# A fused decoder layer in fp32: a pair's products in the order keys, values, queries, and the query features after the sums

## The chip, the cores and the metric

The kernel runs on one core of a Trainium2 chip. The metric is the device time of one execution, in microseconds (us). The core has five engines that run side by side and meet only at semaphores: TensorE (PE, matrix products into PSUM banks), VectorE (DVE), ScalarE (ACT), GpSimd (POOL) and SyncE (SP, which issues the DMAs). Each engine runs its own instructions strictly in the order of the program; an instruction that waits holds everything behind it on its engine.

## What is computed

A decoder layer on x of shape (16, 128, 256): a stack of 8 attention and feed-forward layers, then a cross attention with a context, then a mixture of 8 experts. The change is in the stack alone. For each of the 8 layers:

```python
Q  = elu(x @ Wq + bq) + 1;  Kf = elu(x @ Wk + bk) + 1;  V = x @ Wv + bv   # 16 heads of 64
KV = sum(Kf * V, over the sequence);  sumK = sum(Kf, over the sequence)
att = Q * KV / (Q * sumK + 1e-6)                 # elementwise: one number per channel
x = layernorm(gelu(att @ Wo + bo) + x)
h = gelu(gelu(x @ W1 + b1) @ W2 + b2)            # 256 -> 1024 -> 256
x = layernorm(h + x)
```

The feature elu(u)+1 equals max(u + 1, exp(min(u, 0))), which is how the kernel makes it.

## The kernel before

**Tiles and stages.** The 16 sequences are cut into 4 tiles of 4 sequences (512 tokens); 8 layers times 4 tiles are 32 tiles, numbered g = 0 to 31 in the order in which they run. The 1024 channels of the heads are 8 chunks of 128, handled as 4 pairs p = 0 to 3. Inputs and weights are split into a high and a low part (XTHI and XTLO, WHI and WLO, X1HI and X1LO, W1HI and W1LO), so that one product of a chunk is 6 matmuls of 512 columns, and the product of one kind (keys, values or queries) of a pair is 12.

**A slot.** The function slot exists once for each engine, and slot(l, t) is one step of a software pipeline over three tiles: the projections, features and sums of tile g+1; the output product (Wo), the first layer norm and the hidden layer of tile g; the down product (W2S) and second layer norm of tile g-1. On PE (L819 to L882) a slot runs: pair 0; half of the Wo product (8 chunks for blocks 0 and 2, the last two chunks after a wait for the weighted attention `att` of pair 3); pair 1; the other half of Wo, which completes Y and signals y_mm; pair 2; half of W2S; pair 3; three quarters of the other half of W2S, the transposes of R (the input of the hidden layer), the last quarter; hidden_start (the 8 matmuls of hidden chunks 0 and 1 with X1HI), hidden_rest for these two (4 matmuls with X1LO), the transposes of the input of tile g+2, and hidden chunks 2 to 7.

**Banks.** PS has six PSUM banks: keys in KB = 0 and 1, queries in QB = 2 and 3, values in VB = 4 and 5. A product of the next pair may overwrite its bank only when DVE has used it: keys wait for kf, queries for wq, values for kv_mul. Pairs are called with pair(p, 0, 2, 1): keys, queries, values. The hidden chunks use QB + m % 4: chunks 0 and 1 the two query banks (hidden_start waits for wq of pair 3), 2 and 3 the two value banks (they wait for kv_mul of pair 3), 4 to 7 the same four again behind ACT's gelus.

**ACT, a pair.** clip_keys (two relus of 512 elements from PSUM, L942), clip_queries (two more, L950, then one exponential over keys and queries together, 2048 elements, L954). invert takes the logarithm and the exponential of the denominators (L962, L964), weigh makes att in 8 small instructions (L977). In a slot the order is: invert(3) and weigh(3) of tile g around pair 0; clip_keys(1), invert(0), clip_queries(1), weigh(0); the gelu of Y; pair 2; invert(1); pair 3; weigh(1); invert(2); the copy X1HI (L1054); XTHI (L987); the gelus of the hidden layer with weigh(2) between them. The ACT engine also copies next layer's weights to WHI (high_parts, L923), in one slot of every four two of these just ahead of X1HI.

**DVE, a pair.** features: subtract 1 and add 1 again on the exponentials of the keys (called snap, L1096, from SBUF to SBUF), key features kf (two, L1102), the same for the queries (L1104, and L1108 gives wq, two). sums_of: key features times values, kv_mul (two, L1118), and one reduction over 2048 elements (L1125). denominators: three small instructions, the addition of ES to the query features (L1138), two small ones. newton: two instructions on the inverse (L1150, L1154). The order in a slot, which is written out by hand at L1214 to L1260:

```python
features(nl, nt, 2)
newton(nl, nt, 1)
sums_of(nl, nt, 2, normed1=norm1)        # kv_mul, layer norm of R, then the reduction
denominators(nl, nt, 2)
features(nl, nt, 3)
newton(nl, nt, 2, between=g if tile else None)   # X1LO between its two instructions
sums_of(nl, nt, 3, biased2=...)          # kv_mul, T<-Y,B, then the reduction
denominators(nl, nt, 3)
```

Ahead of it stand pair 0, features of pair 1, T<-Y,BO (called biased, L1174, which waits for y_mm), sums_of and denominators of pair 1, and the residual and the statistics of the first layer norm (L1179 to L1189).

**POOL** does the scale and the shift of both layer norms on 128 x 1024 elements (L663, L665, L700, L702) as soon as DVE has normed, and the low parts of next layer's weights (L626, L638). SP loads weights; none of its work changes.

Of the kernel before, what the change touches and what calls it, by code (L numbers as in the profile page):

```python
# [18 lines left out]
ACT = mybir.ActivationFunctionType  # L19
# [9 lines left out]
TILES = SEQS // TS  # L29
# [417 lines left out]
def attention_stack(nc, X, ident, cross, ffn, a, cross_loads, x, Wkvq, bkvq, Wo, bo, s1, c1, W1, b1, W2, b2, s2, c2):  # L447

    with ExitStack() as ctx:
# [3 lines left out]
        def sem(name):  # L453
            return ctx.enter_context(nc.semaphore(name))
# [42 lines left out]
        KB, QB, VB = 0, 2, 4  # L497
# [11 lines left out]
            sem(n) for n in ("w_hi", "b_neg", "clipped", "ex", "log", "inv", "y_act", "x1_hi", "h_act", "z_act", "xt_hi"))  # L509

# [231 lines left out]
        def _(pe):  # L742
# [49 lines left out]
            def hidden_start(l, t, g):  # L792

                if t == 0:
                    pe.wait_ge(w_lo, (l + 1) * PIECES)
                chunks = (g + 2) * HC if exists(l, t + 1) else LAST * HC
                for m in range(2):
                    pe.wait_ge(wq, chunks - 1 + m)
                    for kc in range(KD):
                        nc.tensor.matmul(PS[:, QB + m, :], W1HI[:, m, kc, :], X1HI[:, kc, :], start=(kc == 0), stop=False)  # L800
                        nc.tensor.matmul(PS[:, QB + m, :], W1LO[:, m, kc, :], X1HI[:, kc, :], start=False, stop=False)

            def hidden_rest(l, t, g, chunks):

                last = (g + 2) * HC if exists(l, t + 1) else LAST * HC
                for m in chunks:
                    if m < 2:
                        for kc in range(KD):
                            ins = nc.tensor.matmul(PS[:, QB + m, :], W1HI[:, m, kc, :], X1LO[:, kc, :], start=False,
                                                   stop=(kc == KD - 1))  # L810
                        ins.then_inc(h_mm, 1)
                        continue
                    if m < 4:
                        pe.wait_ge(kv_mul, last - 3 + m)
                    else:
                        pe.wait_ge(h_act, g * HC + (m - 3))
                    split_product(PS[:, QB + m % 4, :], W1HI[:, m], W1LO[:, m], X1HI, X1LO).then_inc(h_mm, 1)

            def slot(l, t):  # L819
# [13 lines left out]
                pair(0, 0, 2, 1)  # L833
# [9 lines left out]
                pair(1, 0, 2, 1)  # L843
                if tile:
                    down(WO, ATT, (1, 3)).then_inc(y_mm, 1)
                pair(2, 0, 2, 1)
# [9 lines left out]
                pair(3, 0, 2, 1)  # L856
# [59 lines left out]
        def _(act):  # L916
# [9 lines left out]
            def clip_keys(l, t, p):  # L926
# [13 lines left out]
                for i in range(2):  # L940
                    act.wait_ge(k_mm, 2 * n + i + 1)
                    nc.scalar.activation(EX[:, b, 2 + i, :], PS[:, KB + i, :], ACT.Relu, scale=-1.0,  # L942
                                         bias=BNEG[:, 0, 2 * p + i:2 * p + i + 1])

            def clip_queries(l, t, p):
# [8 lines left out]
                nc.scalar.activation(EX[:, b, 2:6, :], EX[:, b, 2:6, :], ACT.Exp, scale=-1.0).then_inc(ex, 1)  # L954
# [39 lines left out]
            def hidden(l, t, g, between, before):  # L994
                if t == 0:
                    act.wait_ge(b1_in, (l + 1) * 16)
                for m in range(HC):
                    act.wait_ge(h_mm, g * HC + (m + 1))
                    nc.scalar.activation(H[:, m, :], PS[:, QB + m % 4, :], ACT.Gelu_apprx_tanh,  # L999
# [88 lines left out]
        def _(dve):  # L1088
# [3 lines left out]
            def features(l, t, p):  # L1092

                n, b = (l * TILES + t) * PAIRS + p, p % 2
                dve.wait_ge(ex, n + 1)
# [4 lines left out]
                for i in range(2):  # L1100
                    c = 2 * p + i
                    nc.vector.scalar_tensor_tensor(EX[:, b, 2 + i, :], PS[:, KB + i, :], BUP[:, 0, c:c + 1],  # L1102
                                                   EX[:, b, 2 + i, :], ALU.add, ALU.max).then_inc(kf, 1)
                nc.vector.tensor_scalar(EX[:, b, 4:6, :], EX[:, b, 4:6, :], -1.0, 1.0, ALU.add, ALU.add).then_inc(snap, 1)  # L1104
# [22 lines left out]
            def denominators(l, t, p):  # L1127
# [6 lines left out]
                nc.vector.reciprocal(ES[:, b, :], sumk).then_inc(stat, 1)  # L1134
                dve.wait_ge(wq, 2 * n + 2)
# [824 lines left out]
```

## Time and profile before

| what | value |
|---|---|
| median of 3 runs | 2939.05 us (2930.69 to 2939.1) |
| the profiled execution's own time | 2939.07 us |
| its span (first to last instruction) | 2937.3 us |
| PE busy | 2820.4 us, 96% |
| DVE busy | 2388.0 us, 81% |
| ACT busy | 1919.4 us, 65% |
| POOL busy | 778.5 us, 27% |
| mean granted clock of TensorE | 0.979 |

The stack takes the span from its start to about 2450 us; cross attention and experts follow. The profile says of each engine how long it worked, but the matmuls are pipelined and their ends are modelled: whether PE waits is read from the distance between the starts of successive matmuls. In the table of the timeline the first number is the start, the second the duration. The chain that ended last is no help here, since it lies in the experts.

### The profile page before, as it was taken

To read this page: it belongs to the slowest core of one execution; us is meant where nothing else is said; L and a number is where in the kernel's file an instruction comes from. 1 tells how busy PE (TensorE), PEld (TensorE's weight loads), DVE (VectorE), ACT (ScalarE), POOL (GpSimd) and SP (SyncE) were. 2 spreads that over 40 slices of the span, in tenths; PEclk is the share of its full clock that TensorE was granted. 3 is DMA by queue.
4 is the path that set the end of the run, shared out by engine and by line. 5 is a ranking of instruction groups with operands and counts; after the bars stand their busy time and mean duration, and the time that the engine had idled before them with its cause. 6 is when DMAs were issued, how large, how long until landed. Compare 5 with 4: busy or idle time off the path is not lost. (4 is left out here: it accounts for less than half of the span.)

```text
span 2937.3 us, 35493 instructions
## 1 busy us (share of the span) xinstructions
PE 2820.4 (96%) x13018; PEld 2331.9 (79%) x13018; DVE 2388.0 (81%) x3583; ACT 1919.4 (65%) x2835; POOL 778.5 (27%) x512
## 2 busy tenths in 40 slices
PE   5799999999999999999999999999999999997989
PEld 4688888888888888888888888888888877775877
DVE  7878898889888988898888888888888875654366
ACT  4667777776777777777777777767767763443255
POOL 4002231223122312321233123312331124432313
PEclk9899999999999999999999999999999999997999
DMA  4000001000100010101010100110010010102322
GB/s 142 1 1 23 24 17 37 22 22 19 36 21 24 19 36 11 33 19 36 12 33 19 37 7 24 32 37 6 22 35 20 1 58 15 50 1 101 122 43 36
DMA packets 62093, 92.00 MB, mean 31 GB/s; under 512 B 16480, under 2 KB 42336, under 8 KB 59744
## 3 DMA queue, kind: packets, MB, share of 16 engines
q1 hardware_dynamic: 57840, 85.46, 9.2%
q0 software_dynamic: 4080, 4.27, 0.9%
q8 instruction: 104, 1.70, 0.2%
q14 instruction: 69, 0.57, 0.1%
HBM read 80.24 MB, written 10.38 MB: 31 GB/s over the span
## 5 line engine op out<-in xcount | busy, mean ns | idle before, releaser
L746 PE MATMUL PS<-XTHI,WHI 128*128 128x512 f32 x1536 | 625.8, 407 | 24.5 <-DVE EX L1102 18.9
L748 PE MATMUL PS<-XTHI,WLO 128*128 128x512 f32 x1536 | 608.1, 396 | 0.0
L747 PE MATMUL PS<-XTLO,WHI 128*128 128x512 f32 x1536 | 603.6, 393 | 0.0
L977 ACT ACTIVATE ATT<-INV,CC,CE 128x128 f32<-128x128 f32 x1024 | 432.4, 484 | 122.7 <-PE Y L788 116.5
L788 PE MATMUL Y<-WO,ATT 128*128 128x256 f32 x2048 | 454.6, 380 | 6.6 <-ACT ATT L977 6.6
L788 PE MATMUL Y<-W2S,H 128*128 128x256 f32 x2048 | 458.0, 379 | 2.0 <-DVE T L1174 1.4
L788 PEld LDWEIGHTS Y<-WO,ATT 128*128 128x128 f32 x2048 | 389.7, 190 | 63.2 <-ACT ATT L977 6.2
L788 PEld LDWEIGHTS Y<-W2S,H 128*128 128x128 f32 x2048 | 386.2, 190 | 56.3 <-DVE T L1174 1.8
L643 POOL TENSOR_TENSOR RSTD<-MV,EPS 128x4 f32<-128x4 f32 x68 | 16.3, 239 | 1346.8 <-DVE MV L1189 1337.5
L746 PEld LDWEIGHTS PS<-XTHI,WHI 128*128 128x128 f32 x1536 | 291.8, 190 | 89.7 <-issue 21.6
L942 ACT ACTIVATE EX<-PS,BNEG 128x512 f32<-128x512 f32 x256 | 165.7, 685 | 299.2 <-DVE INV L1154 156.4
L747 PEld LDWEIGHTS PS<-XTLO,WHI 128*128 128x128 f32 x1536 | 291.7, 190 | 64.7
L748 PEld LDWEIGHTS PS<-XTHI,WLO 128*128 128x128 f32 x1536 | 291.3, 190 | 65.0
L1150 DVE TENSOR_TENSOR EX<-EX,INV 128x1024 f32<-128x1024 f32 x128 | 161.8, 1264 | 164.3 <-ACT INV L964 164.3
L1125 DVE TENSOR_REDUCE SUMS<-EX 128x16 f32<-128x2048 f32 x128 | 292.1, 2282 | 2.3
L954 ACT ACTIVATE EX<-EX 128x2048 f32<-128x2048 f32 x128 | 245.0, 1914 | 4.1
L1138 DVE TENSOR_TENSOR EX<-EX,ES 128x1024 f32<-128x1024 f32 x128 | 223.3, 1744 | 13.7 <-DVE ES L1134 0.5
L962 ACT ACTIVATE INV<-EX 128x1024 f32<-128x1024 f32 x128 | 135.0, 1055 | 109.1 <-DVE EX L1138 108.7
L1096 DVE TENSOR_SCALAR EX<-EX 128x1024 f32<-128x1024 f32 x128 | 138.6, 1083 | 76.3 <-ACT EX L954 76.3
L1102 DVE SCALAR_TENSOR_TENSOR EX<-PS,BUP,EX 128x512 f32<-128x512 f32 x256 | 180.4, 746 | 5.7
L1108 DVE SCALAR_TENSOR_TENSOR EX<-PS,BUP,EX 128x512 f32<-128x512 f32 x256 | 180.5, 747 | 4.6
L999 ACT ACTIVATE H<-PS,B 128x512 f32<-128x512 f32 x256 | 177.5, 694 | 9.4 <-PE PS L748 5.0
(200 smaller groups left out, 4839.1 us busy)
## 6 DMA issues: line engine op xcount, KB each, us to landing
STAGE<-L_attn_Wkvq SPq DMA_DIRECT2D x64, 384.0 KB, 3.2
WO<-L_attn_Wo SPq DMA_DIRECT2D x8, 1024.0 KB, 4.8
W2S<-L_attn_W SPq DMA_DIRECT2D x8, 1024.0 KB, 4.7
STAGE<-L_attn_W SPq DMA_DIRECT2D x32, 256.0 KB, 5.5
WGU<-L_ffn_r_gate SPq DMA_DIRECT2D x8, 512.0 KB, 9.6
WGU<-L_ffn_r_up SPq DMA_DIRECT2D x8, 512.0 KB, 9.7
WD<-L_ffn_r_down SPq DMA_DIRECT2D x8, 512.0 KB, 9.6
rows_in<-R SPq DMA_DIRECT2D x1, 3036.0 KB, 14.0
```

The source lines that it names most:

```text
L746: nc.tensor.matmul(out, whi[:, kc, :], xhi[:, kc, :], start=(kc == 0), stop=False)
L747: nc.tensor.matmul(out, whi[:, kc, :], xlo[:, kc, :], start=False, stop=False)
L748: ins = nc.tensor.matmul(out, wlo[:, kc, :], xhi[:, kc, :], start=False, stop=(kc == KD - 1))
L788: ins = nc.tensor.matmul(Ytm[:, b, :], src[:, c, b * P:(b + 1) * P], w[:, c, :], start=(c == 0), stop=(c == HC - 1))
L942: nc.scalar.activation(EX[:, b, 2 + i, :], PS[:, KB + i, :], ACT.Relu, scale=-1.0, bias=BNEG[:, 0, 2 * p + i:2 * p + i + 1])
L954: nc.scalar.activation(EX[:, b, 2:6, :], EX[:, b, 2:6, :], ACT.Exp, scale=-1.0).then_inc(ex, 1)
L977: ins = nc.scalar.activation(ATT[:, 2 * p + i, ss], INV[:, b, i, ss], ACT.Identity, scale=CE[:, b, k:k + 1], bias=CC[:, b, k:k + 1])
L999: nc.scalar.activation(H[:, m, :], PS[:, QB + m % 4, :], ACT.Gelu_apprx_tanh, bias=B1[:, m:m + 1]).then_inc(h_act, 1)
L1102: nc.vector.scalar_tensor_tensor(EX[:, b, 2 + i, :], PS[:, KB + i, :], BUP[:, 0, c:c + 1], EX[:, b, 2 + i, :], ALU.add, ALU.max).then_inc( ...
L1108: nc.vector.scalar_tensor_tensor(EX[:, b, 4 + i, :], PS[:, QB + i, :], BUP[:, 2, c:c + 1], EX[:, b, 4 + i, :], ALU.add, ALU.max).then_inc( ...
L1125: nc.vector.tensor_reduce(SUMS[:, b, :], by_seq(EX[:, b, 0:4, :]), AX.X, ALU.add).then_inc(sums, 1)
L1138: nc.vector.tensor_tensor(q, q, spread(ES[:, b, :], SEQ), ALU.add).then_inc(denom, 1)
```

## The change

In the stack, and nowhere else:

- PE runs a pair as keys, values, queries (pair(p, 0, 1, 2)). The value banks become 2 and 3, the query banks 4 and 5. The hidden layer's chunks keep banks 2 to 5, so chunks 0 and 1 now lie in the value banks and wait for kv_mul, chunks 2 and 3 lie in the query banks and wait for wq.
- ACT makes the exponential of the keys by itself after the relus of the keys, and that of the queries after the relus of the queries; there are two new semaphores, clipped_k and ex_k.
- On DVE the query half of features becomes query_features and is called from denominators, after the reduction and the reciprocal, ahead of the addition of ES. The order of the calls in the slot stays.

```diff
-        KB, QB, VB = 0, 2, 4
+        KB, VB, QB = 0, 2, 4
+        clipped_k, ex_k = sem("clipped_k"), sem("ex_k")
...
                 for m in range(2):
-                    pe.wait_ge(wq, chunks - 1 + m)
+                    pe.wait_ge(kv_mul, chunks - 1 + m)
...
-                        nc.tensor.matmul(PS[:, QB + m, :], W1HI[:, m, kc, :], X1HI[:, kc, :], start=(kc == 0), stop=False)
-                        nc.tensor.matmul(PS[:, QB + m, :], W1LO[:, m, kc, :], X1HI[:, kc, :], start=False, stop=False)
+                        nc.tensor.matmul(PS[:, VB + m, :], W1HI[:, m, kc, :], X1HI[:, kc, :], start=(kc == 0), stop=False)
+                        nc.tensor.matmul(PS[:, VB + m, :], W1LO[:, m, kc, :], X1HI[:, kc, :], start=False, stop=False)
...
                     if m < 4:
-                        pe.wait_ge(kv_mul, last - 3 + m)
+                        pe.wait_ge(wq, last - 3 + m)
...
-                    split_product(PS[:, QB + m % 4, :], W1HI[:, m], W1LO[:, m], X1HI, X1LO).then_inc(h_mm, 1)
+                    split_product(PS[:, VB + m % 4, :], W1HI[:, m], W1LO[:, m], X1HI, X1LO).then_inc(h_mm, 1)
...
-                pair(0, 0, 2, 1)
+                pair(0, 0, 1, 2)
...
-                    nc.scalar.activation(EX[:, b, 2 + i, :], PS[:, KB + i, :], ACT.Relu, scale=-1.0,
-                                         bias=BNEG[:, 0, 2 * p + i:2 * p + i + 1])
+                    ins = nc.scalar.activation(EX[:, b, 2 + i, :], PS[:, KB + i, :], ACT.Relu, scale=-1.0,
+                                               bias=BNEG[:, 0, 2 * p + i:2 * p + i + 1])
+                ins.then_inc(clipped_k, 1)
+                act.wait_ge(clipped_k, n + 1)
+                nc.scalar.activation(EX[:, b, 2:4, :], EX[:, b, 2:4, :], ACT.Exp, scale=-1.0).then_inc(ex_k, 1)
...
-                nc.scalar.activation(EX[:, b, 2:6, :], EX[:, b, 2:6, :], ACT.Exp, scale=-1.0).then_inc(ex, 1)
+                nc.scalar.activation(EX[:, b, 4:6, :], EX[:, b, 4:6, :], ACT.Exp, scale=-1.0).then_inc(ex, 1)
...
-                dve.wait_ge(ex, n + 1)
+                dve.wait_ge(ex_k, n + 1)
...
+            def query_features(l, t, p):
+
+                n, b = (l * TILES + t) * PAIRS + p, p % 2
+                dve.wait_ge(ex, n + 1)
                 nc.vector.tensor_scalar(EX[:, b, 4:6, :], EX[:, b, 4:6, :], -1.0, 1.0, ALU.add, ALU.add).then_inc(snap, 1)
                 dve.wait_ge(snap, 2 * n + 2)
...
                 nc.vector.reciprocal(ES[:, b, :], sumk).then_inc(stat, 1)
+                query_features(l, t, p)
                 dve.wait_ge(wq, 2 * n + 2)
                 dve.wait_ge(stat, n * 4 + 2)
```

The gelu of the hidden layer (L999) reads its bank as VB + m % 4 instead of QB + m % 4.

## Rows read from the trace of the kernel before

**Rows 1.** Page, busy time of the engines: us, share of the span, instructions
```profile
PE 2820.4 (96%) x13018; PEld 2331.9 (79%) x13018; DVE 2388.0 (81%) x3583; ACT 1919.4 (65%) x2835; POOL 778.5 (27%) x512
```
**Rows 2.** Busy by stretch, one slot: stretch, length, busy by engine, clock, DMA share, GB/s
```profile
1054.88:1128.81 73.93, 73.84 (x338) 61.85 (x336) 65.04 (x97) 52.15 (x77) 12.69 (x8) 1.00 0.06 20
```
**Rows 3.** Timeline of PE, that slot: start us, duration us, engine, line, operation
```profile
1085.00 0.58 PE L746 MATMUL PS<-XTHI,WHI 128*128 128x512 f32 x1
...
1090.69 0.39 PE L746 MATMUL PS<-XTHI,WHI 128*128 128x512 f32 x1
...
1105.85 0.39 PE L746 MATMUL PS<-XTHI,WHI 128*128 128x512 f32 x1
...
1116.38 0.58 PE L800 MATMUL PS<-X1HI,W1HI 128*128 128x512 f32 x1
...
1120.47 0.48 PE L746 MATMUL PS<-X1HI,W1HI 128*128 128x512 f32 x1
...
1128.81 0.39 PE L746 MATMUL PS<-XTHI,WHI 128*128 128x512 f32 x1
```
**Rows 4.** Page, costliest groups, two of ACT: busy us, mean ns of one
```profile
L954 ACT ACTIVATE EX<-EX 128x2048 f32<-128x2048 f32 x128 | 245.0, 1914 | 4.1
...
L962 ACT ACTIVATE INV<-EX 128x1024 f32<-128x1024 f32 x128 | 135.0, 1055 | 109.1 <-DVE EX L1138 108.7
```
**Rows 5.** Timeline of ACT, the same slot and one with weight copies
```profile
1085.47 3.20 ACT L977 ACTIVATE ATT<-INV,CC,CE 128x128 f32<-128x128 f32 x8 [3.82 <-PE Y L788]
...
1106.05 0.69 ACT L950 ACTIVATE EX<-PS,BNEG 128x512 f32<-128x512 f32 x1 [0.68 <-PE PS L748]
...
1108.60 3.17 ACT L977 ACTIVATE ATT<-INV,CC,CE 128x128 f32<-128x128 f32 x8
...
1115.03 1.01 ACT L1054 CAST X1HI<-PS 128x1024 fp32r<-128x1024 f32 x1 [0.89 <-PE PS L866]
...
1189.89 1.55 ACT L923 CAST WHI<-STAGE 128x768 fp32r<-128x768 f32 x2
```
**Rows 6.** Timeline of DVE, the same slot, pairs 1 to 3
```profile
1085.79 1.22 DVE L1174 TENSOR_TENSOR T<-Y,BO 128x1024 f32<-128x1024 f32 x1
...
1088.35 2.29 DVE L1125 TENSOR_REDUCE SUMS<-EX 128x16 f32<-128x2048 f32 x1
...
1090.88 0.20 DVE L1134 RECIPROCAL ES<-SUMS 128x8 f32<-128x8 f32 x1
...
1092.61 1.22 DVE L1179 TENSOR_TENSOR R<-T,X 128x1024 f32<-128x1024 f32 x1
...
1095.40 0.28 DVE L1189 BATCH_NORM_AGGREGATE MV<-ST 128x2 f32<-128x6 f32 x3
...
1098.81 0.68 DVE L1104 TENSOR_SCALAR EX<-EX 128x1024 f32<-128x1024 f32 x1
...
1100.85 1.22 DVE L1150 TENSOR_TENSOR EX<-EX,INV 128x1024 f32<-128x1024 f32 x1
...
1105.85 2.28 DVE L1125 TENSOR_REDUCE SUMS<-EX 128x16 f32<-128x2048 f32 x1
...
1108.82 3.15 DVE L1138 TENSOR_TENSOR EX<-EX,ES 128x1024 f32<-128x1024 f32 x1
...
1117.38 1.22 DVE L1164 TENSOR_TENSOR X1LO<-PS,X1HI 128x1024 fp32r<-128x1024 f32 x1
...
1119.65 1.41 DVE L1118 SCALAR_TENSOR_TENSOR EX<-PS,BA,EX 128x512 f32<-128x512 f32 x2
```
**Rows 7.** Timeline of POOL, the shift of the first layer norm in that slot
```profile
1108.52 2.36 POOL L702 TENSOR_TENSOR R<-R,LN1P 128x1024 f32<-128x1024 f32 x1
```
**Rows 8.** Waits of the whole span: engine, line, waited for, us in total, times, longest
```profile
PE PS L746 <- DVE EX L1102: 18.9, 4, 6.7
```
**Rows 9.** Timeline of PE near the stack's end, a long wait
```profile
2409.59 3.62 PE L788 MATMUL Y<-WO,ATT 128*128 128x256 f32 x10 [3.69 <-ACT ATT L977]
```
**Rows 10.** Busy by stretch just behind that wait: the last but two is the clock
```profile
2410.70:2414.10 3.40, 3.40 (x10) 2.69 (x9) 0.00 (x0) 0.14 (x1) 1.75 (x1) 0.50 1.12 374
```

More of the change, by code:

```diff
@@ L808, in hidden_rest @@
                         for kc in range(KD):
-                            ins = nc.tensor.matmul(PS[:, QB + m, :], W1HI[:, m, kc, :], X1LO[:, kc, :], start=False,
+                            ins = nc.tensor.matmul(PS[:, VB + m, :], W1HI[:, m, kc, :], X1LO[:, kc, :], start=False,
                                                    stop=(kc == KD - 1))
@@ L842, in slot @@
                     down(WO, ATT, (0, 2), range(HC - 2, HC))
-                pair(1, 0, 2, 1)
+                pair(1, 0, 1, 2)
                 if tile:
                     down(WO, ATT, (1, 3)).then_inc(y_mm, 1)
-                pair(2, 0, 2, 1)
+                pair(2, 0, 1, 2)
                 if before:
@@ L855, in slot @@
                     down(W2S, H, (0, 1))
-                pair(3, 0, 2, 1)
+                pair(3, 0, 1, 2)
                 if before:
@@ L998, in hidden @@
                     act.wait_ge(h_mm, g * HC + (m + 1))
-                    nc.scalar.activation(H[:, m, :], PS[:, QB + m % 4, :], ACT.Gelu_apprx_tanh,
+                    nc.scalar.activation(H[:, m, :], PS[:, VB + m % 4, :], ACT.Gelu_apprx_tanh,
                                          bias=B1[:, m:m + 1]).then_inc(h_act, 1)
```

## The prediction, made before the changed kernel ran

> **What bounds the kernel now.** I read the busy times first: PE is busy 96% of the span, DVE 81%, ACT 65% [rows 1]. Busy matmuls say little by themselves, so I took one slot of the stack by stretch and by timeline. It lasts 73.93 us, of which PE is busy 73.84, DVE 65.04 and ACT 52.15 [rows 2]. In it the products follow each other without a hole: from the first start of pair 3's third product to hidden_start 10.53 us, to hidden chunk 2 14.62, to the next slot's first product 22.96 [rows 3]. So in the stack PE sets the pace and nothing else does; whatever the change takes off another engine's path is worth nothing there, and every wait that it puts in front of PE is paid in full, in each of the 31 slots that also project a next tile (g = 0 to 30). What may be gained is the start of the stack, where PE waits for key features, 18.9 us in four waits [rows 8]. DVE has 8.9 us to spare a slot, ACT 21.8 [rows 2]: DVE's order matters nearly as much as PE's.
>
> **The change, part by part.** *The exponential.* One of 1.914 us becomes two of 1.055 [rows 4]: ACT gains 0.2 us of work a pair, 128 times, 25 us in all, beside PE's work. It counts only where ACT's chain is late, below. PE's matmuls and DVE's instructions are the same in number and size.
>
> *Key features earlier.* PE's keys of the next pair no longer wait behind query features. In the steady slot they did not wait, so nothing. At the start the bound is 0 to 18.9 us [rows 8]; half of this comes back, since there the sums and the query features still stand in one DVE queue: I take 9 us of gain.
>
> *Query features later.* wq frees the query banks. It now comes after kv_mul, the reduction and the reciprocal; PE needs it two products after the keys. I follow DVE from the point that anchors it, the moment Y is complete (ACT sees it at 1085.47 [rows 5]). Times are those of the old slot, with PE on time. Of pair 1, DVE has done the key features by then and idles, some 4 us; the queries' part used to fill just this hole. The new run is: biased from 1085.5 (old 1085.79); biased and kv_mul take 2.56 (1085.79 to 1088.35), reduction to end of the reciprocal 2.73 (1088.35 to 1091.08) [rows 6], so 1090.8; then snap and the first wq, about 1.47 of the 2.04 us that the query features take (1098.81 to 1100.85) [rows 6]: 1092.3. PE would start the third product at 1090.69 [rows 3]. **Wait one: 1.65 us.** Behind the waiting product stand the half of W2S and pair 3, all 1.65 later.
>
> DVE goes on without a pause. The rest of the query features ends at 1092.9; ES and the two small ones take 1.43 (of the 1.53 between the reciprocal's end, 1091.08, and 1092.61), residual and statistics 3.07, key features of pair 2 2.04, and newton(1), kv_mul and the norm 5.00 (1100.85 to 1105.85) [rows 6]: the reduction of pair 2 starts at 1104.4 and the query features of pair 2 could start 2.9 later, at 1107.35, with the first wq at 1108.8. But POOL's shift starts 2.67 after the reduction's start, at 1107.07, and lasts 2.36 [rows 7]. Its neighbour in the old trace, the addition of ES, began 0.3 after POOL, and took 3.15 us against 1.22 for the addition of as many elements at 1092.61: it ended 1.09 after POOL's end [rows 6, 7]. Now the snap of the queries stands there. If it is held likewise, it ends at 1109.98, first wq 1110.75. PE is ready for the third product at 1105.85 + 1.65 = 1107.5. **Wait two: 1.3 (not held) to 3.25 us (held).** I take 3.25, for the row is at the same place and of the same engine pair. The two put the third product of pair 3 4.9 us late. The Trainium skill (SBUF — State Buffer, section on SBUF's two separate sides) says that DVE and GpSimd take a shared port pair as an exclusive lock, first come first served; by it the snap is held if POOL starts first, and the 3.15 us agree, and it would be the short wait only if the snap came first.
>
> *ACT after the queries.* Call Q the start of pair 3's third product, now the queries. The last relu can start 2.94 after the start of its product (1106.05 against 1103.11, that is 1105.85 less the 2.74 of a product); the relu takes 0.7 and the exponential 1.06, so weigh(1) starts at Q + 4.65; it takes 3.17 [rows 5] and invert(2) twice 1.06 [rows 4]: Q + 9.95. Only then comes X1HI, 1.01 long [rows 5], Q + 10.95; the transposes are ready before, at Q + 9.2. In the old order ACT had done its exponential one product earlier, and waited 0.89 for PE there [rows 5].
>
> *hidden_start behind kv_mul.* This is the costliest line of the diff. Before, hidden_start waited for wq of pair 3, which DVE made ahead of newton(2). Now it waits for kv_mul of pair 3, and in DVE's order that stands behind newton(2), with X1LO inside it, and X1LO needs X1HI. So the 8 matmuls that were to cover the making of X1LO wait for X1LO and more: X1LO from Q + 11.0, X1LO and the second half of newton 2.27 (1117.38 to 1119.65), first kv_mul 0.74 (of 1.41 for two) [rows 6]: Q + 14.1. PE is there at Q + 10.53. **Wait three: 3.6 us**, even if DVE is otherwise idle; with X1HI as early as before (0.35 us ahead of PE) it would be 2.8.
>
> Then chunk 2, which now takes a query bank: after kv_mul (1.32) come T<-Y,B (1.13), the reduction and reciprocal (2.73), snap and the first wq (1.47): 13.3 + 6.65 = Q + 19.95. PE, 4.09 us after its late hidden_start (1116.38 to 1120.47 [rows 3]), is ready at Q + 18.2. **Wait four: 1.8 us.** From there to the next slot 8.34 us remain, Q + 28.35 against Q + 22.96 before: 5.4 us. DVE's addition of ES and XTLO, 2.7 us, end long before.
>
> *Att of the tile ahead.* ACT's weigh(3) now stands behind the relus of the third product of pair 0. It ends about 13.4 us after the slot's start, when PE comes to the last two chunks of Wo: I take 0; upper bound 0.5 a slot.
>
> *Slots with weight copies.* 7 slots have two copies, 1.55 us, ahead of X1HI [rows 5], now on the path, and POOL's subtractions beside the newtons. Bounds 0 to 5 us; I take 3, or 21 us.
>
> **The sum.** 31 x (4.95 + 5.4) = 321; less 9; plus 21: 333 us. TensorE's clock comes on top: behind a wait of 3.69 us [rows 9] the granted clock was 0.50 for 3.4 us, the 1.2 GHz level [rows 10], which costs half of it, 1.7 us of work. The new slot has two waits of about that size; most of the slow stretch would fall into the slack ahead of the next wait. Bounds 0 to 3.4 us a slot, I take 1: 31 us. From the profiled execution's own 2939.07 us (its span is 1.8 less, and it equals the median) this gives 2939 + 333 + 31 = 3303, rounded **3300 us**, 12% slower; a slot of some 85 us in which DVE's order, not PE, sets the pace.
>
> **The rivals.**
> (1) *The snap slips in ahead of POOL*, wait two is 1.3: 2 us a slot less, 3240 us. For it: the two starts lie 0.3 us apart. Against: POOL starts at a fixed distance from the norm, before the reciprocal is through.
> (2) *The clock falls at both long waits of every slot* and stays down over work that is not slack: 3.4 us a slot instead of 1: 3375 us. The Trainium skill (TensorE: Matmul & The Clock Gate, Part 1) has the half clock as the default that activity lifts; by it this is the case, and rows 10 show the fall after 3.69 us.
> (3) *Only the hidden layer's waits are paid*, since DVE's idle time around Y absorbs the first two: 31 x 5.4 = 167, less 9, plus 10: about 3107. Against: the chain from Y on is all DVE work, 65 us of it in 74.
> (4) *The other side: faster.* If query features were ready before PE comes back to their banks, the early keys would be pure gain: the 18.9 us at the start [rows 8] and the odd waits for kf, up to 2910 us. It decides by one comparison: from Y complete to the first wq, 6.85 us by the rows, must be under the 5.2 us to PE's third product. And kv_mul would have to be ahead of X1LO, which the order of calls excludes.
> (5) *The change doesn't do what it says*: keys' features are early, but no one waits for them in the steady slot; this is contained in the forecast.
>
> **How the numbers follow.** Forecast 0.45; (1) 0.2; (2) 0.17; (3) 0.13; (4) 0.03; the remaining 0.02 for no difference. The range 3190 to 3410 takes in forecast, (1) and (2), with the uncertain start, weight copies and att. A measurement of this kernel tells 0.3%, 9 us, from no change: slower 0.95, same 0.02, faster 0.03.
>
> **What would show it.** After: slots 83 to 88 us apart; on PE waits ahead of L800 (hidden_start) for DVE's L1118 line of about 3.6 us, ahead of hidden chunk 2 and of the third products of pairs 2 and 3 for wq; DVE idle for about 4 us ahead of T<-Y,BO and for several ahead of newton(2); X1HI waiting for ACT, not for PE. A wait at L800 under 2 us, or slots under 78 us, would prove the chain wrong; a clock that stays near 0.98 would strike the last term.

## The result

| kernel | median of its runs | ratio to before, 95% interval | span of the profiled execution | granted clock |
|---|---|---|---|---|
| before | 2939.07 us (2930.69 to 2945.17) | 1 | 2937.3 us | 0.979 |
| after | 3314.43 us (3312.61 to 3316.66) | 1.1284 (1.1260 to 1.1307) | 3314.9 us | 0.943 |

The kernel became 12.8% slower; 3300 us was forecast, in a range of 3190 to 3410. The lines of the changed kernel are numbered up to 10 higher than those of before: L747 is the first matmul of a product (L746 before), L801 is hidden_start (L800), L789 the Wo and W2S products (L788), L1117 gives wq, L1127 gives kv_mul, L1106 gives kf, L1113 is the snap of the queries. The page of after, busy time of the engines (us, share of the span, instructions) and two groups (busy us, mean ns of one, then the idle time ahead and what ended most of it), which answer [rows 1]:

```profile
PE 2930.2 (88%) x13018; PEld 2409.3 (73%) x13018; DVE 2384.8 (72%) x3583; ACT 1956.9 (59%) x2963; POOL 787.7 (24%) x512
...
L747 PE MATMUL PS<-XTHI,WHI 128*128 128x512 f32 x1536 | 654.4, 426 | 174.8 <-DVE EX L1117 151.4
...
L1160 DVE TENSOR_TENSOR EX<-EX,INV 128x1024 f32<-128x1024 f32 x128 | 156.6, 1223 | 495.5 <-ACT INV L968 495.5
```

The work is the same in number, and DVE's is as long as before (2384.8 against 2388.0 us). PE is busy 110 us more with the same 13018 matmuls: some of them ran slower. The last line is the other half of the story: DVE, whose order now sets the pace, stands idle for 495.5 us itself ahead of the first half of newton, waiting for ACT (164.3 us on the page of before).

The waits of PE from 200 to 2700 us (engine, line, waited for, us in total, times, longest):

```profile
PE PS L747 <- DVE EX L1117: 148.8, 80, 4.7
PE PS L801 <- DVE EX L1127: 114.4, 29, 5.7
```

Neither row exists in the trace of before. They are 263.2 us, 9.1 us a slot; 29 slots of the stack lie in this stretch. Where they stand in one slot is read from the timeline of PE (start us, duration us, operation, in brackets the idle time ahead and its releaser), against [rows 3]:

```profile
1084.65 0.50 PE L747 MATMUL PS<-XTHI,WHI 128*128 128x512 f32 x1 [1.30 <-DVE EX L1117]
...
1103.26 0.50 PE L747 MATMUL PS<-XTHI,WHI 128*128 128x512 f32 x1 [3.16 <-DVE EX L1117]
...
1107.39 5.69 PE L789 MATMUL Y<-W2S,H 128*128 128x256 f32 x24
...
1118.85 0.77 PE L801 MATMUL PS<-X1HI,W1HI 128*128 128x512 f32 x1 [3.17 <-DVE EX L1127]
1119.41 0.63 PE L802 MATMUL PS<-X1HI,W1LO 128*128 128x512 f32 x1
1119.84 0.63 PE L801 MATMUL PS<-X1HI,W1HI 128*128 128x512 f32 x1
...
1122.10 1.08 PE L810 MATMUL PS<-X1LO,W1HI 128*128 128x512 f32 x4
...
1124.53 0.50 PE L747 MATMUL PS<-X1HI,W1HI 128*128 128x512 f32 x1 [0.48 <-DVE EX L1117]
...
1170.23 0.50 PE L747 MATMUL PS<-XTHI,WHI 128*128 128x512 f32 x1 [1.33 <-DVE EX L1117]
```

The first and the last row are the third product of pair 2 in two slots running: a slot of 85.58 us, against 73.93 [rows 2], 11.65 more. The four waits are the four of the prediction, in its order: one (third product of pair 2), two (third product of pair 3), three (hidden_start), four (hidden chunk 2). From 1103.26 on they are 3.16, 3.17, 0.48 and 1.33, together 8.14 us. The remaining 3.5 us are slower matmuls in the main: the queries' product of pair 3 took 4.13 us (1103.26 to 1107.39) instead of 2.74, and hidden_start's eight 3.25 (1118.85 to 1122.10) instead of 2.27, X1LO's wait included (1116.38 to 1118.65 before). Some 1.1 us is left. Part of it is in how brackets count, from the modelled end of the matmul ahead, which lies behind the next possible start: ahead of waits one and two the starts lie 1.70 and 3.56 us apart instead of 0.23, 0.17 more than the bracket each time. For four waits that is 0.7 us, an estimate; 0.4 stay open. Busy by stretch of after (stretch, length, busy and instructions of PE, PEld, DVE, ACT, POOL, clock, DMA share, GB/s), for a slot, behind wait two, and behind wait three:

```profile
1047.19:1132.88 85.69, 77.58 (x337) 64.08 (x336) 65.58 (x96) 55.32 (x87) 16.44 (x11) 0.96 0.08 27
1103.20:1107.40 4.20, 4.14 (x13) 3.26 (x14) 4.09 (x8) 0.69 (x1) 0.00 (x0) 0.68 0.59 179
1118.80:1122.10 3.30, 3.25 (x8) 2.65 (x9) 3.30 (x3) 0.00 (x0) 0.00 (x0) 0.55 0.00 0
```

The granted clock, 1.00 in a slot of before [rows 2], falls behind both long waits of this slot; matmuls of 512 columns then start 0.43 us apart (1119.41 to 1119.84) instead of 0.23.

**The whole difference.** The last two chunks of Wo of the first slot start at 95.88 us before and at 98.92 after, those of the slot behind the 31st at 2409.59 and 2793.91. So 3.0 us come from ahead of this point of the first slot, 381.3 us from the 31 slots, 12.3 each, and 6.7 us are given back behind them, where the code is the same (before's own runs differ by more than that). One slot in four has the two weight copies: a layer of four slots takes 348.2 us (mean of seven layers), 5.9 more than four of 85.6, where before's 299.0 us was 3.3 more than four of 73.9. Slots without copies are 85.5 to 86.6 us long in the changed kernel.

### The profile page after: what moved, and what is told of

The parts are those of the page before. It is cut to its first block and busy times, and to the rows that moved or that the text cites. A ratio compares the mean times of both kernels' runs of the same rounds, so it can differ in the third digit from the quotient of the medians.

```text
span 3314.9 us, 35621 instructions
## 1 busy us (share of the span) xinstructions
PE 2930.2 (88%) x13018; PEld 2409.3 (73%) x13018; DVE 2384.8 (72%) x3583; ACT 1956.9 (59%) x2963; POOL 787.7 (24%) x512
## 3 DMA queue, kind: packets, MB, share of 16 engines
HBM read 80.24 MB, written 10.38 MB: 27 GB/s over the span
## 5 line engine op out<-in xcount | busy, mean ns | idle before, releaser
L747 PE MATMUL PS<-XTHI,WHI 128*128 128x512 f32 x1536 | 654.4, 426 | 174.8 <-DVE EX L1117 151.4
L749 PE MATMUL PS<-XTHI,WLO 128*128 128x512 f32 x1536 | 627.8, 409 | 0.0
L748 PE MATMUL PS<-XTLO,WHI 128*128 128x512 f32 x1536 | 625.7, 407 | 0.0
L1160 DVE TENSOR_TENSOR EX<-EX,INV 128x1024 f32<-128x1024 f32 x128 | 156.6, 1223 | 495.5 <-ACT INV L968 495.5
L747 PEld LDWEIGHTS PS<-XTHI,WHI 128*128 128x128 f32 x1536 | 303.7, 198 | 267.8 <-DVE EX L1117 179.4
L789 PE MATMUL Y<-WO,ATT 128*128 128x256 f32 x2048 | 457.4, 382 | 8.4 <-ACT ATT L981 8.4
L789 PE MATMUL Y<-W2S,H 128*128 128x256 f32 x2048 | 462.0, 382 | 2.0 <-DVE T L1184 1.4
L789 PEld LDWEIGHTS Y<-WO,ATT 128*128 128x128 f32 x2048 | 389.2, 191 | 68.0 <-ACT ATT L981 12.9
L789 PEld LDWEIGHTS Y<-W2S,H 128*128 128x128 f32 x2048 | 391.4, 192 | 57.4 <-DVE T L1184 1.8
L749 PEld LDWEIGHTS PS<-XTHI,WLO 128*128 128x128 f32 x1536 | 304.0, 198 | 69.3
L954 ACT ACTIVATE EX<-PS,BNEG 128x512 f32<-128x512 f32 x256 | 171.8, 683 | 307.1 <-PE PS L749 305.3
L748 PEld LDWEIGHTS PS<-XTLO,WHI 128*128 128x128 f32 x1536 | 304.7, 198 | 65.6
L943 ACT ACTIVATE EX<-PS,BNEG 128x512 f32<-128x512 f32 x256 | 169.0, 685 | 269.7 <-PE PS L749 260.6
L801 PE MATMUL PS<-X1HI,W1HI 128*128 128x512 f32 x128 | 74.0, 578 | 128.3 <-DVE EX L1127 128.3
L1106 DVE SCALAR_TENSOR_TENSOR EX<-PS,BUP,EX 128x512 f32<-128x512 f32 x256 | 180.4, 746 | 5.7
L1117 DVE SCALAR_TENSOR_TENSOR EX<-PS,BUP,EX 128x512 f32<-128x512 f32 x256 | 180.4, 746 | 4.5
L1164 DVE SCALAR_TENSOR_TENSOR INV<-EX,INV 128x1024 f32<-128x1024 f32 x128 | 179.1, 1399 | 3.3
L1113 DVE TENSOR_SCALAR EX<-EX 128x1024 f32<-128x1024 f32 x128 | 181.0, 1414 | 0.0
```

Source lines behind the costliest of these rows:

```text
L747: nc.tensor.matmul(out, whi[:, kc, :], xhi[:, kc, :], start=(kc == 0), stop=False)
L748: nc.tensor.matmul(out, whi[:, kc, :], xlo[:, kc, :], start=False, stop=False)
L749: ins = nc.tensor.matmul(out, wlo[:, kc, :], xhi[:, kc, :], start=False, stop=(kc == KD - 1))
L789: ins = nc.tensor.matmul(Ytm[:, b, :], src[:, c, b * P:(b + 1) * P], w[:, c, :], start=(c == 0), stop=(c == HC - 1))
L954: ins = nc.scalar.activation(EX[:, b, 4 + i, :], PS[:, QB + i, :], ACT.Relu, scale=-1.0, bias=BNEG[:, 2, 2 * p + i:2 * p + i + 1])
L1117: nc.vector.scalar_tensor_tensor(EX[:, b, 4 + i, :], PS[:, QB + i, :], BUP[:, 2, c:c + 1], EX[:, b, 4 + i, :], ALU.add, ALU.max).then_inc( ...
```

## The experiments

The theory: DVE's order sets the time, through two things that PE waits for, wq behind the sums and kv_mul behind newton and X1LO; the clock is a small extra. The rivals: one of the two carries nearly all; the new product order or the split exponential has a cost of its own; the clock is a large part.

### Query features back in their place, or kv_mul moved forward, or both

Edit A (e2, in the changed kernel: wq as early as before) and edit B (e1: kv_mul of pair 3 ahead of newton(2) and X1LO); e7 has both.

```diff
 # A, in features and denominators
+                query_features(l, t, p)        # at the end of features
...
-                query_features(l, t, p)        # after the reciprocal
 # B, in the slot of DVE; key_values is the kv_mul loop of sums_of
                     features(nl, nt, 3)
+                    key_values(nl, nt, 3)
                     newton(nl, nt, 2, between=g if tile else None)
-                    sums_of(nl, nt, 3, biased2=(l, t, g, tile) if before else None)
+                    sums_of(nl, nt, 3, biased2=(l, t, g, tile) if before else None, products=False)
```

> The changed kernel with the sums no longer ahead: query features stand right behind the key features again (order keys, values, queries and the two exponentials are kept). Theory: the waits for wq (third product of pairs 2 and 3, hidden chunk 2) vanish, 1.3 + 3.2 + 0.5 us; the wait ahead of hidden_start stays, since kv_mul of pair 3 is still behind X1LO and X1HI still behind ScalarE's weigh(1) and invert(2): 3.2 to 3.6 us a slot. 31 x 3.5 = 108 us over the kernel before: about 3050 us, 3035 to 3080. Rival (the later query product alone is harmless, all the loss is the sums' place): within 1% of 2939 us.

> The changed kernel with one edit: on VectorE the two kv_mul of pair 3 are made ahead of newton(2), so hidden_start no longer stands behind X1LO. Theory (a chain on VectorE and ScalarE sets each slot; the last of its waits is the one for wq of pair 3): the wait ahead of hidden_start falls from 3.2 to about 0.5 us, but the wait ahead of hidden chunk 2 grows from 0.5 to some 3 us, because wq of pair 3 comes only 1.3 us earlier (the two kv_mul no longer stand between X1HI and it). Slot 1.3 us shorter, 31 x 1.3 = 40 us: about 3275 us, 3255 to 3295. Rival (the wait for kv_mul is itself the price): 31 x 3.3 = 102 us less, about 3210 us.

> Keys, values, queries and two exponentials, but the query features right behind the key features and the kv_mul of pair 3 ahead of newton(2) and X1LO: both waits for VectorE are taken away, only X1HI behind ScalarE's weigh(1) and invert(2) is left. Theory: ahead of hidden_start some 0.5 us a slot (1.5 to 2 in the slots with weight copies), no wait elsewhere in the steady slot, start 5 to 15 us earlier: 2940 to 2965 us. Rival (the later query product costs by itself, by way of ScalarE): above 3000 us.

| kernel | median | ratio to before, 95% interval | a slot without copies |
|---|---|---|---|
| after | 3314.43 us | 1.1284 (1.1260 to 1.1307) | 85.5 to 86.6 us |
| A (e2) | 3084.44 us | 1.0506 (1.0480 to 1.0532) | 78.5 to 78.9 us |
| B (e1) | 3338.72 us | 1.1381 (1.1355 to 1.1407) | 85.6 to 88.0 us |
| A and B (e7) | 2936.56 us | 1.0019 (1.0006 to 1.0031) | 73.8 to 74.5 us |

The slots are given from the shortest to the longest; two of A's, of 80.1 and 80.2 us, are left out. The waits of PE in A (first row) and with A and B (the others), 200 to 2700 us:

```profile
PE PS L801 <- DVE EX L1128: 120.0, 30, 5.7
```

```profile
PE PS L801 <- ACT X1HI L1058: 10.9, 7, 1.6
PE PS L747 <- DVE EX L1128: 5.9, 7, 1.2
```

With A the waits for wq are gone, and what is left is hidden_start's wait for kv_mul (L1128 there). With both these two rows are all that is left of them, in the seven slots with weight copies, and the time is that of before within 0.3%. So the two moves on DVE take away the whole loss against before: the query features go back to their old place, and kv_mul goes ahead of where before had it, for in before too it stood behind newton(2) and X1LO, only nothing of hidden_start waited for it. The new product order, the banks and the split exponential stay in e7. These are not quite free: e5 below, with the split exponential alone, is 28 us faster than e7, and the 16.8 us of waits in the slots with copies are most of that.

B alone is a miss: 3275 was expected, and it came out slower than the changed kernel. The timeline of PE in e1, the two long waits:

```profile
1103.82 0.80 PE L747 MATMUL PS<-XTHI,WHI 128*128 128x512 f32 x1 [3.16 <-DVE EX L1117]
...
1124.03 0.58 PE L747 MATMUL PS<-X1HI,W1HI 128*128 128x512 f32 x1 [3.83 <-DVE EX L1117]
```

Kv_mul came early, and hidden_start no longer waits; but the next thing late on the same chain is wq for chunk 2, and its wait grew from 0.48 to 3.83 us. That is 0.2 us more than the two waits that it replaces (3.17 and 0.48), where a slot is 0.8 us longer in the mean of seven layers (87.87 against 87.04, slots with copies included). What else changed is where the slow matmuls lie. The stretches behind the two waits in e1:

```profile
1104.00:1108.00 4.00, 4.00 (x11) 3.19 (x12) 3.90 (x8) 0.69 (x1) 0.00 (x0) 0.60 0.63 186
1124.00:1128.00 4.00, 3.97 (x10) 3.12 (x11) 3.23 (x5) 1.22 (x2) 0.00 (x0) 0.57 0.01 2
```

In the changed kernel the second slow stretch falls on hidden_start, whose delay only shortens wait four. In e1 it falls on the hidden chunks, with nothing left to shorten behind them. The changed kernel's own trace has a slot that shows the first half of this, the one with pair 2 at 1249.34 us. Its hidden_start meets the full clock:

```profile
1290.84 0.47 PE L801 MATMUL PS<-X1HI,W1HI 128*128 128x512 f32 x1 [3.48 <-DVE EX L1127]
...
1296.52 0.51 PE L747 MATMUL PS<-X1HI,W1HI 128*128 128x512 f32 x1 [1.80 <-DVE EX L1117]
```

```profile
1290.80:1294.10 3.30, 3.26 (x16) 2.74 (x17) 3.30 (x3) 0.00 (x0) 0.00 (x0) 1.00 0.00 0
```

From hidden_start to chunk 2 it is 5.68 us here, and 5.68 as well in the slot above with its clock of 0.55 (1118.85 to 1124.53): what the slow matmuls take, wait four gives back. Only where the stretch is longer does it cost something: in 8 of the 31 slots the distance is 6.1 to 6.5 us. The second half, e1, was a guess from a pair of traces, so it got its own run.

### Is it the clock? Keeping PE at work through the wait

e8 is e1 plus, in each slot, 14 matmuls of 512 columns into the bank Y while it is free, ahead of chunk 2. It adds work, and the wait of PE ends at the same semaphore.

```diff
+                    if m == 2 and at_least(l, t, 1) and exists(l, t + 1):
+                        pe.wait_ge(z_b, g)
+                        for k in range(14):
+                            nc.tensor.matmul(Y[:, 0:TOK], W1HI[:, 0, 0, :], X1HI[:, 0, :], start=True, stop=True)
```

> The run with kv_mul ahead of X1LO (3339 us), and on TensorE, behind a wait for T<-Y,B, 14 matmuls of 512 columns into the free bank Y ahead of hidden chunk 2; their results are overwritten unused. They take 3.2 us and lie in the 3.9 us in which TensorE waits there for wq. Theory (the run before it was slower than the changed kernel because the stretch at 1.2 GHz now falls on the 36 hidden matmuls, which are on the path, and no longer on the 8 of hidden_start, which were not): the granted clock there stays at 2.4 GHz, the slot is about 1.7 us shorter, 31 x 1.7 = 53: about 3285 us, 3265 to 3300, below the changed kernel too. Rival (the order of VectorE's work costs it, not the clock): 3339 us or more, by the added matmuls.

It took 3257.07 us (3255.84 to 3272.91), ratio 1.1128 (1.1101 to 1.1154): 82 us less than e1, and less than the 3265 to 3300 expected. The mean slot of seven layers is 85.17 us against 87.87; the slot shown here is 82.97 against 86.07. Timeline of PE in e8, the third product of pair 3, the added matmuls, chunk 2:

```profile
1077.78 0.50 PE L747 MATMUL PS<-XTHI,WHI 128*128 128x512 f32 x1 [3.15 <-DVE EX L1121]
...
1092.46 3.49 PE L817 MATMUL Y<-X1HI,W1HI 128*128 128x512 f32 x14
...
1096.44 0.51 PE L747 MATMUL PS<-X1HI,W1HI 128*128 128x512 f32 x1 [0.49 <-DVE EX L1121]
```

Clock behind the first of these waits, and over 400 us:

```profile
1078.00:1082.00 4.00, 4.00 (x19) 3.33 (x19) 3.90 (x8) 1.80 (x3) 0.00 (x0) 1.00 0.59 183
...
1000.00:1400.00 400.00, 372.07 (x1654) 306.14 (x1653) 307.92 (x443) 264.28 (x401) 93.28 (x56) 0.99 0.07 22
```

3.34 us of the wait became useless work and the kernel got faster, so the slow matmuls behind the waits were real time. Behind chunk 2 the full pace holds in every slot of e8. Behind the third product, where nothing was put, it holds in only 9 of the 23 slots without copies, the one shown above among them. The very next slot has the slow stretch:

```profile
1160.64 0.50 PE L747 MATMUL PS<-XTHI,WHI 128*128 128x512 f32 x1 [3.03 <-DVE EX L1121]
```

```profile
1160.70:1164.70 4.00, 4.00 (x11) 3.19 (x12) 3.90 (x7) 0.69 (x1) 0.00 (x0) 0.59 0.02 4
```

The waits there are the same in all (3.0 to 3.2 us, once 3.4), and the slots are 82.8 to 83.0 us long where the clock stayed up; of the others ten are 84.1 to 84.8 and the last ones, with a longer slow stretch, 85.3 to 85.4. So one slow stretch costs 1.3 to 1.8 us of slot, 2.4 where it is longest, in one and the same kernel; two of them are the 3.1 us between the slots of 86.07 and 82.97, and in the mean of all slots filling the one wait gave 2.7 us, with 1.7 expected. The Trainium skill (TensorE: Matmul & The Clock Gate, Part 1) has half speed as the default and full speed as what activity keeps up; e8 agrees, in that activity put into one wait kept the full clock behind it. Why the other stretch recovers in some slots and not in others is not shown by any run.

### POOL's hold on the snap

In e4 POOL scales and shifts 8 of 256 channels of the first layer norm only; the other channels go unscaled and unshifted, so this part of the computation is left out.

```diff
-                    nc.gpsimd.tensor_tensor(r, r, bcast(LN1P[:, 0, :], TS), ALU.mult).then_inc(x1_s, 1)
+                    nc.gpsimd.tensor_tensor(r[:, :, 0:8], r[:, :, 0:8], bcast(LN1P[:, 0, 0:8], TS), ALU.mult).then_inc(x1_s, 1)
...
-                    nc.gpsimd.tensor_tensor(r, r, bcast(LN1P[:, 1, :], TS), ALU.add).then_inc(x1, 1)
+                    nc.gpsimd.tensor_tensor(r[:, :, 0:8], r[:, :, 0:8], bcast(LN1P[:, 1, 0:8], TS), ALU.add).then_inc(x1, 1)
```

> The changed kernel, with GpSimd's scale and shift of the first layer norm applied to 8 of 256 channels only (that part of the computation is left out): no long GpSimd instruction runs beside the query snap of pair 2. Theory (the snap is held by GpSimd's shift): the snap of pair 2 takes 0.65 instead of 2.8 us, the wait ahead of pair 3's third product falls from 3.2 to about 1.2 us, the slot is 2.0 us shorter, and a shorter wait lets the clock fall less often there, another 0 to 1.4 us: 3314 - 62 - (0 to 43) = 3210 to 3252 us. Rival (the snap is slow for another reason, or the wait is covered elsewhere): 3300 to 3315 us.

3202.34 us (3200.92 to 3206.78), ratio 1.0915 (1.0889 to 1.0941), 112 us under the changed kernel. The snap of the queries of pair 2 and the product behind it, in the changed kernel (POOL's shift first) and in e4:

```profile
1099.53 2.35 POOL L703 TENSOR_TENSOR R<-R,LN1P 128x1024 f32<-128x1024 f32 x1
...
1099.63 2.79 DVE L1113 TENSOR_SCALAR EX<-EX 128x1024 f32<-128x1024 f32 x1
1102.46 1.41 DVE L1117 SCALAR_TENSOR_TENSOR EX<-PS,BUP,EX 128x512 f32<-128x512 f32 x2
```

```profile
1141.14 0.65 DVE L1113 TENSOR_SCALAR EX<-EX 128x1024 f32<-128x1024 f32 x1
...
1142.62 0.50 PE L747 MATMUL PS<-XTHI,WHI 128*128 128x512 f32 x1 [0.77 <-DVE EX L1117]
```

POOL starts 0.10 us ahead, the snap lasts 2.79 us and ends at 1102.42, 0.54 after POOL; without POOL it lasts 0.65. Wait two goes from 3.16 to 0.77. The snap was held for 2.78 to 2.80 us in all 30 slots of the changed kernel. Most slots of e4 without copies are 81.8 to 82.0 us long, 3.7 less, of which the wait explains 2.4; the rest is the slow queries' product (4.13 us instead of 2.74), which is gone with the long wait. The Trainium skill (SBUF — State Buffer, section on SBUF's two separate sides) calls the port pair that DVE and GpSimd share an exclusive lock, and the pair of rows agrees with it: 0.65 us alone, 2.79 behind POOL's start. What no run separates is whether the length of the hold, or only its place right ahead of wq, could be mended.

### One part alone, in the kernel before

e5 has only the exponential of the keys by itself, with kf waiting for ex_k and the queries' part for ex; e6 only the product order and banks; e3 only the query features after the sums.

```diff
 # e5, in features of before
-                dve.wait_ge(ex, n + 1)
+                dve.wait_ge(ex_k, n + 1)
...
+                dve.wait_ge(ex, n + 1)        # ahead of the queries' snap
 # e3, in denominators of before
                 nc.vector.reciprocal(ES[:, b, :], sumk).then_inc(stat, 1)
+                query_features(l, t, p)
```

> The kernel before with only the exponential taken apart: ScalarE makes the exponential of the keys ahead of the relus of the queries, VectorE makes the key features as soon as it is there and waits for the queries' exponential behind them; product order and place of the sums are the old ones. Theory: TensorE is full in the steady slot, ScalarE's 25 us more work lie beside it, so only the start can gain: the four waits for key features there (18.9 us) shrink by about half, 2925 to 2935 us. Rival (two short exponentials and two waits cost on the path): 2945 us or more.

> The kernel before with only the product order keys, values, queries and its banks; one exponential behind the queries, features in the old place. Theory: it has the wait ahead of hidden_start of the run with the queries before the sums (3.6 us), and on top the one exponential of 1.91 instead of 1.06 us behind the last product, on the way to X1HI and to the weighted attention of pair 3: 0.9 us and up to 0.9 us more a slot. 3084 + 31 x 0.9 to 1.8 = 3112 to 3140 us. Rival (the exponential's split does not matter): 3084 us.

> The kernel before with only one part of the change: query features after the sums (order keys, queries, values and the one exponential stay). Theory: now the queries are the second product of a pair and need wq of the pair before one product earlier, 4.4 us late in pair 2 and 4.1 more in pair 3; hidden_start needs wq of pair 3, which stands behind X1LO, newton, kv_mul, T and the reduction: 21.9 us after the third pair's query product against 13.3 at which TensorE is there, 8.6 us. Slot 17 us longer, 31 x 17 = 530 us: about 3470 us, 3430 to 3520, slower than the changed kernel. Rival (the products' order is what costs, the sums' place does not): near 2939 us.

| kernel | median | ratio to before, 95% interval |
|---|---|---|
| e5, exponential | 2908.09 us (2900.32 to 2914.65) | 0.9927 (0.9914 to 0.9941) |
| e6, product order | 3205.19 us (3204.80 to 3215.67) | 1.0935 (1.0918 to 1.0951) |
| e3, sums ahead | 3670.55 us (3660.30 to 3671.40) | 1.2509 (1.2482 to 1.2537) |

**e5** is faster than both kernels, and by more than the 2925 to 2935 expected. Timeline of PE ahead of hidden chunk 2, before and then e5:

```profile
1113.78 1.22 PE L866 MATMUL PS<-ident,R 128*128 128x128 f32 x8
1114.83 1.89 PE L788 MATMUL Y<-W2S,H 128*128 128x256 f32 x8
```

```profile
1099.25 1.04 PE L867 MATMUL PS<-ident,R 128*128 128x128 f32 x8
1100.12 1.89 PE L789 MATMUL Y<-W2S,H 128*128 128x256 f32 x8
1101.66 0.58 PE L801 MATMUL PS<-X1HI,W1HI 128*128 128x512 f32 x1
...
1105.39 0.47 PE L747 MATMUL PS<-X1HI,W1HI 128*128 128x512 f32 x1
```

The transposes of R write the banks of the keys, so they wait for kf. Before, they took 1.05 us from start to start, and the kf of pair 3 ended at about 1114.29, in their middle; in e5 it ended at 1098.27 and they took 0.87. From hidden_start to chunk 2 it is 3.73 us instead of 4.09 [rows 3], since X1HI and X1LO follow the transposes. That is 0.5 us a slot of the regular kind (73.40 against 73.93) in two holes too small to bear a bracket; and the wait of the transposes for kf, 1.47 us once in a layer (16.9 us in 16 over the whole span, 4.83 of it in the first slot), shrinks to 5.8 us in 2. A layer is 295.3 us against 299.0; 8 times this is 30 us, and the profiled spans differ by 38.7, the medians of the same chip by 23.

**e6** was expected at 3112 to 3140 us. The two waits that it was made for came, at hidden_start and for att; a wait at the second product (the values, whose bank waits for kv_mul one product sooner) and the clock (0.96 over 1000 to 1400 us) were left out of that expectation. Timeline of PE:

```profile
1187.66 1.99 PE L789 MATMUL Y<-WO,ATT 128*128 128x256 f32 x8 [0.62 <-ACT ATT L978]
...
1223.50 0.50 PE L747 MATMUL PS<-XTHI,WHI 128*128 128x512 f32 x1 [0.77 <-DVE EX L1125]
1241.40 0.77 PE L801 MATMUL PS<-X1HI,W1HI 128*128 128x512 f32 x1 [4.33 <-DVE EX L1125]
```

**e3** is the worst of all: with the old product order the queries' banks are wanted one product sooner, and hidden_start waits for wq of pair 3, the last result of DVE's new queue. Three waits of a slot, timeline of PE:

```profile
1205.94 0.76 PE L746 MATMUL PS<-XTHI,WHI 128*128 128x512 f32 x1 [4.05 <-DVE EX L1112]
...
1226.78 0.80 PE L746 MATMUL PS<-XTHI,WHI 128*128 128x512 f32 x1 [3.80 <-DVE EX L1112]
...
1250.07 0.76 PE L800 MATMUL PS<-X1HI,W1HI 128*128 128x512 f32 x1 [8.29 <-DVE EX L1112]
```

Direction and places were right, the size 200 us too small: this slot of 99.1 us is 25.2 over before's (in the mean of seven layers it is 23.5), of which waits are about 18.9, one of them at pair 1 (0.7 to 2.1 us by its brackets) not foreseen, and the rest, about 6.3, I put down to the slow clock, which was left out of that expectation. The parts do not add: e3 and e6 alone lose 734 and 274 us against before on their chips, and the whole change 375. The new product order gives the late wq one product more, and so mends most of what e3 breaks.

## Why the prediction was right

By its own steps, per regular slot:

| term | forecast | measured |
|---|---|---|
| wait one | 1.65 us (its own times give 1.6) | 1.30 to 1.33 |
| wait two | 3.25, if not held 1.3 | 3.16 held; 0.77 without POOL (e4) |
| wait three | 3.6 | 3.17 |
| wait four | 1.8 | 0.48 behind a slow hidden_start, 1.80 behind one at full clock |
| clock | 1, bounds 0 to 3.4 | 1.4 to 1.7 behind wait two; 1.0 behind wait three, mostly given back by wait four |
| slots with copies | 3 a layer more | 2.6 (5.9 less 3.3) |
| keys early in the steady slot | 0 | 0.5 in e5 |
| att of the tile ahead | 0, at most 0.5 | no wait in regular slots |
| start of the stack | -9 us | about +3 |
| sum | 333 + 31 = 364 us | 375 |

**The mechanism held.** DVE's idle time ahead of biased was forecast at some 4 us and is 3.02, ahead of newton(2) at several and is 7.10; X1HI waits for ACT's own queue. DVE in that part of the slot, in the changed kernel:

```profile
1114.55 1.23 DVE L1160 TENSOR_TENSOR EX<-EX,INV 128x1024 f32<-128x1024 f32 x1 [7.10 <-ACT INV L968]
1115.69 1.22 DVE L1174 TENSOR_TENSOR X1LO<-PS,X1HI 128x1024 fp32r<-128x1024 f32 x1
1116.83 1.22 DVE L1164 SCALAR_TENSOR_TENSOR INV<-EX,INV 128x1024 f32<-128x1024 f32 x1
1117.96 1.41 DVE L1127 SCALAR_TENSOR_TENSOR EX<-PS,BA,EX 128x512 f32<-128x512 f32 x2
```

kv_mul needs nothing of the three instructions ahead of it. It stands behind them in the queue, and hidden_start behind it: a 3.17 us wait of PE during which DVE first idled 7.10 us. That e7 is level with before shows that the loss needs this or the place of wq.

**Wait four and the clock belong together.** The prediction put the slow stretch in "the slack ahead of the next wait", and priced what is left of it at 1 us. Half of that was right: behind wait three it falls on hidden_start, which starts chunk 2 as late as wq comes anyway, so wait four shrank from 1.8 to 0.48 and the part from hidden_start on cost what it should; where the clock stayed up (1290.84 to 1296.52) it is 1.80, just as forecast, and the distance the same 5.68. Behind wait two it fell on the queries' product, and this is not slack: ACT's last relu of the queries needs the end of it. Timeline of ACT:

```profile
1107.63 0.69 ACT L954 ACTIVATE EX<-PS,BNEG 128x512 f32<-128x512 f32 x1 [1.87 <-PE PS L749]
1108.35 1.06 ACT L958 ACTIVATE EX<-EX 128x1024 f32<-128x1024 f32 x1
1109.31 3.17 ACT L981 ACTIVATE ATT<-INV,CC,CE 128x128 f32<-128x128 f32 x8
...
1114.43 0.99 ACT L1058 CAST X1HI<-PS 128x1024 fp32r<-128x1024 f32 x1
```

With Q = 1103.26 the last relu starts at Q + 4.37, not at Q + 2.94, weigh(1) at Q + 6.05 instead of 4.65, X1HI at Q + 11.17 instead of 9.95. ACT is on the path from there through X1LO and kv_mul, so 1.2 to 1.4 us of a slower PE went through three engines and came back as a later hidden_start (PE, late too, saw a wait of 3.17 instead of 3.6). The slot at 1249.34 us has the forecast's terms apart: waits of 1.30, 3.04, 3.48 and 1.80, 9.6 us by the brackets and 10.3 with 0.17 for each (an estimate), against the 10.3 that the prediction's four make; and a queries' product of 4.45 us instead of 2.74, 1.7 for the clock. The step that was mis-sized is "most of the slow stretch would fall into the slack ahead of the next wait": 1 us was taken, and the one stretch that is not slack costs 1.4 to 1.7. A slot is 11.65 or 11.77 us longer, against 11.35 forecast without the copies.

The sum is close in part by offsets. By the spans the loss is 377.6 us against 364: the slots without the copies took some 11 us more than the forecast's 352, the start 12 more, the copies 3 less (18 for 21), and 6.7 came back behind the stack, where nothing was forecast.

**The two that were wrong outright.** "In the steady slot they did not wait, so nothing" was read off a list of waits. The wait was there, two holes of 0.2 and 0.4 us that the modelled ends cover in before; only distances between starts show them. And the list of before itself has 16 waits of the transposes for kf, 16.9 us, 1.47 of them once in a layer ahead of a slot's hidden_start, which [rows 8] and the prediction's bound leave out:

```profile
PE PS L866 <- DVE EX L1102: 16.9, 16, 4.8
```

They shrink in e5. The start of the stack did not gain either. The key features of the first four pairs did come 1.4 to 3.2 us earlier, but the waits for them [rows 8] only fell from 18.9 to 15.1 us, and four waits for wq, 8.1 us, came on top; the last two chunks of Wo of the first slot start 3.0 us later, and in that slot hidden_start waited 10.38 us for kv_mul.

**The rivals.** That the snap slips in ahead of POOL (3240) needed a start 0.10 us earlier, and would have been worth up to 3.7 us a slot by e4; that the clock stays down at both waits (3375) is what happened as to places, but behind wait three it stays down over work that mostly is slack; that only the hidden layer's waits are paid (3107) falls with waits one and two, and e2 puts the queries' part at 230 us of the 375. Of the other side there is e5: the gain that the early key features hold is 0.7%, and the change gave it away.

## What to carry over

On an engine that runs in order, moving a step later moves everything that waits for it: take the first consumer on the bottleneck engine, and add up the queue between the point that anchors it and the new place; these sums were right to 0.5 us, once the clock's share is taken apart. Do not let a result that frees a bank (kv_mul) stand behind instructions that themselves wait for another engine. And price a wait on a PE that was full as its length plus the slow matmuls behind it, asking of these what reads their result: a wait that is moved, as in e1, can cost more than one that stays.

## What the hardware showed beyond that

- Waits of 3.16 and 3.17 us in an otherwise full stream of matmuls brought the granted clock to 0.68 and 0.55 over the next 3 to 4 us, where 3.69 us had been seen before [rows 9, 10]; behind waits of 1.30 and 0.48 us it stayed at 1.00. Yet with the other wait of the slot filled, in e8, waits of 3.0 to 3.2 us left the clock up in 9 of 23 slots and not in the rest, and in the changed kernel it stayed at 1.00 behind a wait of 3.48: the length of one wait does not decide it.
- 14 matmuls a slot that compute nothing, 3.49 us by their row, made a kernel 82 us faster.
- A slow stretch of matmuls cost 1.3 to 1.8 us where a chain of other engines read their result, and nothing where another wait stood behind it (5.68 us from hidden_start to chunk 2 at a clock of 0.55 and of 1.00).
- A DVE instruction on 128 x 1024 elements from SBUF to SBUF took 0.65 us alone and 2.79 beside a POOL instruction that had started 0.10 us earlier.
- Without any brackets in a list of waits a slot still held 0.5 us of waiting, 17 us of the stack.
